# The attention output product in fp16 halves, its row sums one step later, and an fp32 fifth chunk in both feed-forward stages

## The reference

```
x = x + 0.5 * ffn(layernorm(x))
x = x + attention(layernorm(x))
x = x + 0.5 * ffn(layernorm(x))

attention: q, k, v = projections of x with biases
  scores = q k^T / sqrt(256), taken as |scores|, causal, softmax
  out = (weights v) Wo^T + bo
ffn: mixed = three-tap mix of x along the sequence
  h = mixed W1 + b1 for 9 paths of 64; paths = h W2 + b2
  one path per row, the argmax of tanh(mixed Wo1 + bo1) Wo2 + bo2
  layernorm(x + the chosen path) * gamma + beta
```

## Time and profile before

| | |
|---|---|
| median of three runs | 1492.32 us (1491.56 to 1492.96) |
| the profiled execution, its time | 1492.41 us |
| its span, first to last instruction | 1490.6 us |
| granted PE clock, mean | 0.972 |
| busy PE / DVE / ACT / POOL | 91 / 79 / 63 / 22% |
| `ffn(0)` | 0 to about 298 us |
| attention, batches 0 and 1 | about 300 to 745, and 745 to 1192 us |
| `ffn(1)` | about 1193 us to the end |

### The profile page before, as it was taken

How to read it: one execution, slowest core, us unless ns; L and a number is a source line. 1 busy time by engine, 2 the same in 40 slices (tenths; PEclk the granted TensorE clock), 3 DMA queues, 4 the chain that set the end, 5 groups by cost and what they waited for, 6 DMA issues and landing times.

```text
span 1490.6 us, 25905 instructions
## 1 busy us (share of the span) xinstructions
PE 1354.3 (91%) x7636; PEld 781.1 (52%) x7636; DVE 1176.9 (79%) x2343; ACT 935.8 (63%) x1749; POOL 322.5 (22%) x359
## 2 busy tenths in 40 slices
PE   3999999958999999998968999999998959999994
PEld 2567776634455454544434455454544435666663
DVE  5999998766777777778867778777778857999986
ACT  5666766265566767665755566767666766777752
POOL 2255544430101000000040101000000023555422
PEclk9999999979999999999979999999999959999998
DMA  5143433210010000103010011000103021343221
GB/s 154 50 122 107 118 104 93 87 57 1 29 44 30 14 28 1 44 0 114 1 45 1 29 44 34 9 28 1 44 0 114 0 73 42 100 117 106 90 78 57
DMA packets 86994, 82.26 MB, mean 55 GB/s; under 512 B 8539, under 2 KB 86884, under 8 KB 86884
## 3 DMA queue, kind: packets, MB, share of 16 engines
q1 hardware_dynamic: 86884, 80.91, 18.3%
HBM read 55.43 MB, written 25.46 MB: 54 GB/s over the span
## 4 chain that ended last, share of the span: by engine, by line
PE 65%; DVE 15%; issue 10%; ACT 6%; POOL 2%; DMA 1%; DVEq 0%; ACTq 0%; POOLq 0%; SPq 0%
PE PS L1407 57%; PE PS L1602 3%; PE PS L1415 2%; DVE R L795 2%; DVE R L840 2%; DVE R L780 1%; DVE R L973 1%; DVE R L846 1%; DVE st L711 1%; DVE R L803 1%; ACT R L1257 1%; PE PS L1476 1%; ACT R L1294 1%; PE PS L1503 1%; ACT R L1298 1%
## 5 line engine op out<-in xcount | busy, mean ns | idle before, releaser
L1407 PE MATMUL PS<-R 128*128 128x512 f16 (+3 forms) x3456 | 713.7, 361 | 29.2 <-DVE R L973 19.4
L1407 PEld LDWEIGHTS PS<-R 128*128 128x128 f16 (+1 forms) x3456 | 325.6, 98 | 394.6 <-DVE R L973 35.4
L973 DVE TENSOR_TENSOR R<-R 128x512 f16<-128x512 f32 (+3 forms) x288 | 188.5, 655 | 112.5 <-ACT R L1298 111.1
L1285 ACT ACTIVATE R<-PS 128x512 f32 (+5 forms) x288 | 160.1, 558 | 165.1 <-PE PS L1407 164.6
L1407 PE MATMUL PS<-w_hi,R 128*128 128x256 f16 x1152 | 212.0, 274 | 9.7 <-DVE R L786 8.6
L1294 ACT ACTIVATE R<-R 128x512 f32 (+4 forms) x288 | 169.5, 589 | 51.0 <-DVE R L967 49.5
L1407 PE MATMUL PS<-R,w_hi 128*128 128x512 f16 x640 | 197.1, 390 | 4.4 <-DVE R L780 4.4
L967 DVE TENSOR_TENSOR R<-R,max_row 128x512 f32 (+4 forms) x288 | 187.0, 650 | 7.4 <-ACT max_row L1331 7.4
L1298 ACT ACTIVATE R<-R 128x512 f16<-128x512 f32 (+3 forms) x288 | 171.1, 594 | 26.4
L545 POOL TENSOR_SCALAR veps<-mv 128x4 f32<-128x4 f32 x48 | 13.4, 279 | 804.1 <-DVE mv L718 661.3
L961 DVE TENSOR_TENSOR run_max<-run_max,R 128x512 f32<-128x512 f32 (+3 forms) x272 | 173.9, 639 | 9.3 <-DVE run_max L961 1.7
(11 more groups left out here) (116 smaller groups left out, 1644.7 us busy)
## 6 DMA issues: line engine op xcount, KB each, us to landing
R<-x_scratch SPq DMA_DIRECT2D x48, 512.0 KB, 4.6
x_scratch<-R SPq DMA_DIRECT2D x32, 512.0 KB, 3.1
R<-oh_scratch SPq DMA_DIRECT2D x32, 320.0 KB
R<-in_L_attn_x SPq DMA_DIRECT2D x16, 512.0 KB, 5.0
R<-oh_scratch SPq DMA_DIRECT2D x32, 256.0 KB
out<-R SPq DMA_DIRECT2D x16, 512.0 KB, 3.1
R<-in_L_ffn_W SPq DMA_DIRECT2D x2, 288.0 KB
R<-in_L_ffn_W SPq DMA_DIRECT2D x1, 512.0 KB
```

The lines of the kernel that those rows point to most:

```text
L973: v.tensor_tensor(p_lo[:, i * TT + lo:(i + 1) * TT], pf[:, (i % 2) * TT + lo:(i % 2 + 1) * TT], p_hi[:, i * TT + lo:(i + 1) * TT], ALU.sub ...
L1285: a.activation(cols(ring, ring_m + i * TT + lo, TT - lo), ps_s[:, i, lo:], ACT.Abs, scale=1.0 / (QS * XS * D ** 0.5)).then_inc(abs_done, 1)
L1407: ins = t_.matmul(dst, w, xx, start=start and n == 0, stop=stop and n == last, skip_group_check=skip)
```

## The change

Four things are changed.

1. `U` becomes `U_hi` and `U_lo`, both fp16, scaled by 2^-19. ACT writes `U_hi` in one operation of 1024 columns; DVE then writes `U_lo` from `ps_u` and `U_hi` (`weighted_low`), and it is DVE that releases `u_done`. `weighted_low` stands behind the second maximum at the start of a step, in step 7 behind the reduce, and at the end of a batch behind the first of the next batch's statistics.
2. `wvo` becomes `wvo_hi` and `wvo_lo`, scaled by 64 like the other weights, and each output product six fp16 products in place of two fp32 ones. Folding gets two more DVE operations.
3. The row sums leave `output`. Those of tiles 0 to 5 are made in the first block of the first pair of the step after that in which the outputs were; those of tile 6 behind the first pair of step 7. At the end of a batch their order stays.
4. `whole` holds for the fifth chunk in both feed-forward stages, so `ffn(1)` too multiplies it in fp32, and its third group of halves is not made.

```diff
-        U = a3.take(DC * TT)
+        U_hi = a3.take(DC * TT, F16)
+        U_lo = a3.take(DC * TT, F16)
...
         def whole(ph, c):
 
-            return ph == 0 and c == LAST
+            return c == LAST
...
-                v.memset(wvo[:, :, D:D + 8], 1.0 / (D * BETA))
+                v.memset(wvo_hi[:, :, D:D + 8], WS / (D * BETA))
+                v.memset(wvo_lo[:, :, D:D + 8], 0.0)
...
+                wvo_f = wo_s.rearrange("p (c d) -> p c d", c=DC)
                 for c in range(DC):
 
-                    ins = v.scalar_tensor_tensor(out=wvo[:, c, 0:D], in0=bo_b[:, :], scalar=1.0 / (D * BETA),
+                    ins = v.scalar_tensor_tensor(out=wvo_f[:, c, :], in0=bo_b[:, :], scalar=1.0 / (D * BETA),
                                                  in1=PS[:, 6, c * D:(c + 1) * D], op0=ALU.mult, op1=ALU.add)
+                ins.then_inc(wvo_step, 1)
+                dve.wait_ge(wvo_step, 1)
+                v.tensor_scalar(wvo_hi[:, :, 0:D], wvo_f, WS, None, ALU.mult).then_inc(wvo_step, 1)
+                dve.wait_ge(wvo_step, 2)
+                ins = v.scalar_tensor_tensor(out=wvo_lo[:, :, 0:D], in0=wvo_f, scalar=WS, in1=wvo_hi[:, :, 0:D],
+                                             op0=ALU.mult, op1=ALU.subtract)
...
+                def weighted_low(j):
+
+                    dve.wait_ge(u_hi_done, b * NT + j + 1)
+                    v.scalar_tensor_tensor(out=U_lo, in0=ps_u.rearrange("p c s -> p (c s)"), scalar=US, in1=U_hi,
+                                           op0=ALU.mult, op1=ALU.subtract).then_inc(u_done, 1)
+
                 def output(s, u, rows=xr):
...
-                    if u >= 1:
-                        output_sums(s, u - 1, rows)
-                    if u == SUB - 1:
-                        output_sums(s, u, rows)
-
...
                     def first(i):
+                        if has_o(j) and i == 1:
+                            weighted_low(j - 1)
...
                     def first_pair(i):
+                        if i == 0:
+                            for u in range(SUB):
+                                output_sums(s - 2, u, xr)
                         if is_int(j, NT - 1):
                             for u in ((), (0, 1), (2,), (3,), ())[i]:
                                 output(s - 1, u, xr_beside)
+                            if i == SUB:
+                                for u in range(SUB):
+                                    output_sums(s - 1, u, xr_beside)
...
+                    else:
+                        weighted_low(j - 1)
                     over_pairs(dve, j, pair)
...
                 first_stats(b + 1, range(1))
+                weighted_low(NT - 1)
                 for u in range(SUB):
                     output(b * NT + NT - 1, u)
+                    if u >= 1:
+                        output_sums(b * NT + NT - 1, u - 1, xr)
+                output_sums(b * NT + NT - 1, SUB - 1, xr)
...
-                    a.activation(U[:, 0:TT], ps_u[:, 0, :], ACT.Copy)
-                    a.activation(U[:, TT:], ps_u[:, 1, :], ACT.Copy).then_inc(u_done, 1)
+                    a.activation(U_hi, ps_u.rearrange("p c s -> p (c s)"), ACT.Copy, scale=US).then_inc(u_hi_done, 1)
...
-                    for c in range(DC):
-                        ins = t_.matmul(ps_x[:, u % 2, 0:D + 1], U[:, c * TT + u * P:c * TT + (u + 1) * P],
-                                        wvo[:, c, 0:D + 1], start=c == 0, stop=c == DC - 1)
+                    ins = split_product(ps_x[:, u % 2, 0:D + 1],
+                                        [((cols(U_hi, c * TT + u * P, P), cols(U_lo, c * TT + u * P, P)),
+                                          (wvo_hi[:, c, 0:D + 1], wvo_lo[:, c, 0:D + 1])) for c in range(DC)],
+                                        True, True)
```

More of the change, by code:

```diff
@@ L27 @@
 BETA = 1.0 / 16
+US = 2.0 ** -19
 P_LOG = 8.317766166719343
@@ L142, in macaron @@
         wqk_lo = sb("wqk_lo", [P, DC, D], F16)
-        wvo = sb("wvo", [P, DC, D + 8])
+        wvo_hi = sb("wvo_hi", [P, DC, D + 8], F16)
+        wvo_lo = sb("wvo_lo", [P, DC, D + 8], F16)
         wo2 = sb("wo2", [DM + 1, NP])
@@ L215, in macaron @@
         sub_done, exp_done, phi_done, plo_done = sem("sub_done"), sem("exp_done"), sem("phi_done"), sem("plo_done")
+        u_hi_done, wvo_step = sem("u_hi_done"), sem("wvo_step")
         pv_done, u_done, out_psum, rden_done = sem("pv_done"), sem("u_done"), sem("out_psum"), sem("rden_done")
@@ L369, in whole @@
         def whole(ph, c):
-            return ph == 0 and c == LAST
+            return c == LAST
         def groups_before(ph, t):
-            return t * (len(GROUPS) - 1) if ph == 0 else NTT * (len(GROUPS) - 1) + t * len(GROUPS)
+            return use(ph, t) * (len(GROUPS) - 1)
         def masked_chunk(t, c, n=1):
@@ L704, in _ @@
             dve.sem_inc(plo_done, 2)
+            dve.sem_inc(u_done, 1)
             dve.sem_inc(spare_free[0], 1)
@@ L1098, in _ @@
             act.sem_inc(abs_done, SUB)
-            act.sem_inc(u_done, 1)
             def ffn(ph):
```

## The result

The changed kernel takes 1475.03 us (median of five runs, 1472.9 to 1477.0) beside 1491.6 for the kernel before on the same chip: a ratio of 0.9885, with a 95% interval of 0.9872 to 0.9899. A second series gave 1473.79 beside 1492.52, ratio 0.9876 [0.9862, 0.9891]. So 16.6 to 18.7 us went, where the forecast had 10.9.

A forecast was written before the change was run, and what follows sets the result against it. PE, busy 91% of the span, was taken as the bound. Terms -8.4 - 3.2 + 0.7 - 1.3 + 1.6 - 0.5 = -11.1 took 1492.4 to 1481.3 us, stated as 1481.5; range 1475 to 1489.

The forecast's parts named there:

- Output product, -8.4: Attention, steps 1 to 5: each output product takes 0.66 us instead of 0.87, so 40 of them save 8.4 us.
- Moved sums, -3.2: Attention, steps 2 to 4: row sums leave the step's end, so PE's waits for max_col go; 3.2 us saved.
- Step 1, +0.7: Step 1 of each batch: no idle DVE time hides the low half; 0.35 us late per batch, 0.7 lost.
- Steps 6 and 7, -1.3: Last two steps of a batch: shorter products and earlier maxima, less DVE's added sums; about 0.65 us per batch, 1.3 saved.
- End of a batch, +1.6: After the last value products: the low half follows ACT's copy, PE idles 2.4 us instead of 1.26; twice 0.8 lost.
- SP's queue, 0: Stores and residual loads: sums come about 7 us into the next step, but rows are needed much later; cost 0.
- Fifth chunk, -0.5: Second feed-forward stage, 16 tiles: fp32 costs PE 0.42 us more per tile, DVE and ACT do less; net 0.5 saved.
- The first turn 0.4: First turn of the second feed-forward stage: the fp32 fifth chunk loses 0.4 us there.
- (a): Rival, chance 0.12: PE bounds every turn of the second feed-forward stage, the fp32 chunk loses 6.7 us; 1488.5 us.
- (b): Rival, chance 0.06: DVE bounds step starts, value products start up to 2.46 us later in 14 steps; up to 1515 us.
- (c): Rival, chance 0.06: six fp16 output products take PE as long as two fp32 ones; near 1491 us.
- (d): Rival, chance 0.10: all PE savings arrive, steps 6 and 7 give 2.9, key steps 3.5, none late; about 1476 us.

## Why the prediction was wrong, and where it was right

- **Output product, -8.4: right.** 0.66 for 0.87; steps 2 to 5 shorter by 0.83 each with this part alone.
- **Moved sums, -3.2: right, a little low.** `max_col` waits are gone in steps 2 and 3 and 0.16 in step 4; steps 2, 3 and 4 are 1.41, 1.44 and 1.43 shorter, that is 0.6 each beyond the products and 3.6 in six. With the sums back, 2.4 a batch return in steps 0 to 6, which is 1.8 from these three and 0.6 from step 6.
- **Step 1, +0.7: right in sign.** PE waits 0.31 for `p_low` there, where it was 0.06 before and 0.3 more was forecast; net the step is 0.58 shorter where 0.49 was worked out. In steps 2 to 6 such waits are 0.2 at most.
- **Steps 6 and 7, -1.3: about right.** Step 6 is 0.93 shorter, 1.9 in two. Step 7's waits before the end were 4.98 in sum and are 5.82, 0.77 of it the wait for the low half that the forecast left out; the four shorter products pay for that. The wait for `max_col` is 0.36 shorter there, where 0.5 was forecast.
- **End of a batch, +1.6: about right.** PE waits 2.46 as forecast (2.4), and step 7 with the end is 0.95 longer a batch. The lower clock, left to the range, came in 5 of 14 such waits; in one of them it made the stretch to DVE's statistics 61.65 for 60.61, and over the five it cost 1.0 to 1.3 a time and not 1.8.
- **SP's queue, 0: right.** No wait of DVE for the residual rows was seen.
- **Fifth chunk, -0.5: this step failed, in the price of its first turn and in the clock, which it put at nothing.** Four of its five parts held: the fp32 chunk costs PE 1.72 a tile (1.73), a turn takes 15.56 (15.54), nine turns lose 0.91 (1.0), and the last turns gain 0.62 and 1.19 (1.8 together) where the clock stays. "The first turn 0.4" lost was wrong in sign: I took PE's added work as the price of that turn, and didn't ask what the removed copy stood in front of on ACT. It gained 1.3. And I looked for the clock only behind the wait that the change makes longer, and not behind the two that it makes shorter; there each traced execution of the kernel before lost another 1.5 to 1.8. Together -3.6 to -3.9 between the traces, -5.5 in the medians with this part alone.

Whether -3.9 and -5.5 differ at all is open: the interval of the second begins at 3.3. One more gain shows in part of the traces. In two of the six traces without the fp32 chunk (the first one of the changed kernel without it, and that of the kernel with the third group moved) DVE's low half of the mixed rows, line 794 here, takes 1.5 us in place of 1.2 in some turns, PE then waits 0.42 for `result` and not 0.13, and the turns from choice 3 to 15 lose 0.9 to 1.1 in sum. DVE in two turns of the first of these:

```profile
1264.95 1.21 DVE L794 TENSOR_TENSOR R<-R 128x1024 f16<-128x1024 f32 x1
...
1280.39 1.51 DVE L794 TENSOR_TENSOR R<-R 128x1024 f16<-128x1024 f32 x1
```

In the second stage of the eight traces with the fp32 chunk no such long operation was seen, and the nine steady turns take 139.95 in all eight. Why the operation is longer at times no run shows.

The forecast fell 5.7 to 7.8 us short. By the traces, 3.1 to 3.4 of it are the fifth chunk and 0.8 attention; the rest is not assigned.

Of the rivals, (a) fell: PE's price of four thirds is there, 1.72 for 1.31, so the rule of the Trainium skill (FP8 and Floating Point Precision, TensorE Precision Notes) holds for the engine, yet a steady turn lost only 0.10, and the ramp and the tail gained more. (b) fell because the cover held: no wait for `p_low` at the start of steps 2 to 6 grew by more than 0.1. (c) fell with the first row. (d) gave the nearest time, 1476, mostly by luck: of its reasons only the 3.5 of the steps with key statistics came true (3.6); steps 6 and 7 did not give 2.9, step 1 was late, and the ramp of the second stage was not among them.

## What to carry to other kernels

When an edit removes an instruction, list what it stood in front of on its engine, turn by turn, and above all while a pipeline fills: a copy of 0.6 us that waits 1.7 for its input delays everything behind it, needed or not. Where an order is written by hand, moving such an operation behind the work that others wait for can bring most of what removing it brings (3.9 us here, beside 5.5 for the removal in all turns). And price a wait of PE with what may follow it: here waits of about 2 us and more cost another 1 to 3 in some executions where PE was the bound, those of up to 1.93 never.

## What the runs showed of the hardware

The granted clock's answer to one and the same wait of PE (2.45 for `th`, 2.59 for `result`) differed between two executions of one program, and the two answers were swapped. In 14 traces it fell behind none of 198 waits of 1.0 to 1.93 us that began at the full clock, behind 8 of 39 of 1.95 to 2.09, behind 11 of 25 of 2.45 to 2.6 and behind all 61 over 2.7. A drop behind the waits of 2.45 to 2.6 cost 1.0 to 3.2 us; behind the wait of 1.99 in step 7 it cost nothing. By these costs a place with such a wait scatters by about 1.5 us from one execution to the next, an estimate from the 1.46 and 1.75 of the two traces of the kernel before.
